# Score matmuls on four parts of the array, with a new order of the token pipeline, two buffers for h and staggered first weights

## What is computed

```
x = x + layernorm(attention(layernorm(x)))
x = x + layernorm(experts(layernorm(x)))

attention, token by token: 16 heads, 32 + 16 (rotary) numbers each; the scores are head against head
    within one token:  einsum("bsid,bsjd->bsij", q, k), softmax over j, einsum("bsij,bsjd->bsid", attn, v), @ Wo + bo
    q from a latent of 128, k and v from another; rotary part of k from x
experts: 64 experts of width 192, the best 6 for each token, at most 128 tokens to an expert,
    plus a shared gate/up/down of width 384
```

## Time and profile before

| | |
|---|---|
| median of 3 runs | 2026.46 us (2020.72 to 2035.89) |
| profiled execution | 2029.77 us, span 2027.8 us |
| TensorE, VectorE, ScalarE, GpSimd busy | 93%, 75%, 54%, 27% of the span |
| granted TensorE clock, mean | 0.975 |
| DMA packets | 414103, 289704 of them under 512 B |

### The profile page before, as it was taken

One profiled execution on the slowest core, in us unless ns is written; L12 is line 12 of the kernel. 1 busy time (PEld: TensorE's weight loads), 2 busy tenths in 40 slices (PEclk: granted clock), 3 DMA queues, 4 the chain that ended last, 5 costly groups with the idle time before them and its releaser, 6 DMA issues. The chain is left out here.

```text
span 2027.8 us, 49115 instructions
## 1 busy us (share of the span) xinstructions
PE 1893.7 (93%) x14529; PEld 1504.8 (74%) x14529; DVE 1520.7 (75%) x3935; ACT 1091.5 (54%) x1745; POOL 550.1 (27%) x773
## 2 busy tenths in 40 slices
PE   5899999999999999999999999985899999988886
PEld 4788888888888888888888888874454555546664
DVE  6588888888888888888888888773444444429997
ACT  4576767666666767666666767651222233223333
POOL 1111112111111112111111111110344444427776
PEclk8799999999999999999999999997899999999998
DMA  5245454545454454545455554437999999979994
GB/s 189 69 129 147 128 153 129 151 128 150 124 143 138 133 150 128 150 129 152 126 140 137 137 146 128 140 108 222 334 299 284 274 310 307 291 202 394 406 398 171
DMA packets 414103, 383.99 MB, mean 189 GB/s; under 512 B 289704, under 2 KB 298024, under 8 KB 413992
## 3 DMA queue, kind: packets, MB, share of 16 engines
q1 hardware_dynamic: 393504, 324.98, 53.1%
q0 software_dynamic: 14336, 35.66, 7.5%
q10 hardware_dynamic: 6208, 22.68, 2.9%
HBM read 232.46 MB, written 150.63 MB: 189 GB/s over the span
## 5 line engine op out<-in xcount | busy, mean ns | idle before, releaser
L861 POOL TENSOR_SCALAR ve<-mv 128x1 f32<-128x1 f32 x192 | 42.7, 222 | 1073.1 <-DVE mv L698 1072.3
L593 ACT COPY qT<-bank 48x512 f32<-48x512 f32 x256 | 269.1, 1051 | 72.2 <-PE bank L445 67.6
L593 ACT COPY kT<-bank 48x512 f32<-48x512 f32 x256 | 268.8, 1050 | 4.8
L1068 PE MATMUL e_gu<-w,xgT 128*128 128x384 f32 x512 | 184.3, 503 | 15.4 <-DMA w<-w_ed 13.5
L452 PE MATMUL bank<-wgu,xfT 128*128 128x416 f32 x512 | 189.1, 369 | 8.3 <-ACT xfT L593 8.3
L453 PE MATMUL bank<-wgu,xfT 128*128 128x416 f32 x512 | 183.5, 358 | 0.0
L642 ACT ACTIVATE prob<-prob 128x512 f32<-128x512 f32 x128 | 78.7, 633 | 176.3 <-DVE prob L795 176.3
L469 PEld LDWEIGHTS score_ps<-kT,qT 48*64 48x64 f32 x4096 | 133.4, 138 | 40.7 <-issue 40.7
L469 PE MATMUL score_ps<-kT,qT 48*64 48x64 f32 x4096 | 151.1, 225 | 11.5 <-ACT kT L593 11.5
L1068 PEld LDWEIGHTS e_gu<-w,xgT 128*128 128x128 f32 x512 | 93.2, 192 | 74.7 <-DMA w<-w_ed 14.2
L1229 DVE SCALAR_TENSOR_TENSOR tanh<-tanh,e_gu 128x192 f32<-128x192 f32 x64 | 22.7, 354 | 166.3 <-ACT tanh L1155 166.3
(11 more groups left out here) (177 smaller groups left out, 4922.8 us busy)
## 6 DMA issues: line engine op xcount, KB each, us to landing
w<-w_eg SPq DMA_DIRECT2D x60, 768.0 KB, 6.7
acc_scratch<-zero SPq DMA_DIRECT2D x130, 256.0 KB, 4.2
w<-w_ed SPq DMA_DIRECT2D x60, 384.0 KB, 11.0
xf_scratch<-xf SPq DMA_DIRECT2D x64, 288.0 KB, 2.1
xin<-x SPq DMA_DIRECT2D x64, 256.0 KB, 2.9
v_scratch<-v SPq DMA_DIRECT2D x64, 256.0 KB, 3.7
vbd<-v_scratch SPq DMA_DIRECT2D x128, 128.0 KB, 3.2
o_scratch<-o SPq DMA_DIRECT2D x256, 64.0 KB, 2.3
```

The costliest lines, as they stand in the source:

```text
L593: nc.scalar.copy(dst, src).then_inc(done.sem, 1)
L1068: last = nc.tensor.matmul(gu_ps[par], xgT[:, par, n, :], w1[:, place, n, :], start=(n == 0), stop=(n == KD - 1))
```

## The change

Six things change together. (1) q and k go to SBUF on two sets of partitions, 0 to 47 and 64 to 111, for the first and the last 64 tokens of a tile; `scores` then has matmuls on four parts of the array (two of rows, r, by two of columns, g), all 32 in one piece, the two row parts writing to different banks. `spread` makes 16 copies of 48 x 256 for 8 of 48 x 512. q is laid out by (head, token) within four tokens, so o's partitions are (head, token), and the mask changes to p % B4. (2) o is written to memory in that order, and oin is read back by four DMAs, one for each token of the four, each of 32 partitions x 16 x 32 numbers, where there was one DMA of 128 x 512. (3) TensorE's order: the latent product is split into its high part and its low part, with the transposes of k between; q's product goes ahead of the gate/up products; the second gate/up half goes behind the transposes of oin; xn is transposed ahead of prob; the rank matmul goes last. (4) The orders of ScalarE and VectorE follow; yn becomes VectorE's last. (5) h has two buffers. (6) The first experts' weights are asked for one expert a round, in the rounds NT + 1 to NT + 4.

The diff, cut to its core:

```diff
-    c[:, C_NEG:C_NEG + B4] = np.where((p[:, None] // H) % B4 == np.arange(B4), 0.0, -BIG)
+    c[:, C_NEG:C_NEG + B4] = np.where(p[:, None] % B4 == np.arange(B4), 0.0, -BIG)
...
-        qT, kT = qT_all[0:DQ], kT_all[0:DQ]
+        qT = qT_all[:, 0:P // 2, :].rearrange("p (c x) y -> p c (x y)", x=B4).rearrange("p c (h t) -> p c h t", t=B4)
+        kT = kT_all[:, 0:P // 2, :]
...
-        h = sb("h", [P, SI])
+        h = sb("h", [P, 2, SI])
...
-                    dst = o_d[1 - par].rearrange("(c g b t) (h d) -> g b (t h) c d", c=8, g=2, b=2, h=H)
+                    dst = o_d[1 - par].rearrange("(c g b) (x d) -> g b x c d", c=8, g=2, b=2, d=DH)
                     src = o[:].rearrange("p (c b d) -> p b c d", c=8, b=2)
                     for g in range(2):
                         for b in range(2):
                             sp.dma_start(dst[g, b], src[64 * g:64 * g + 64, b]).then_inc(o_out.sem, 16)
                     sp.wait_ge(o_out.sem, o_out.at(i - 3))
+                    settle(sp)
                     sp.wait_ge(pe_oT.sem, pe_oT.at(i - 4))
-                    sp.dma_start(oin[:], o_d[1 - par]).then_inc(o_in.sem, 16)
+                    settle(sp)
+                    src = o_d[1 - par].rearrange("c (h t d) -> t c h d", t=B4, d=DH)
+                    for n in range(B4):
+                        sp.dma_start(oin[n:P:B4, :].rearrange("p (h d) -> p h d", d=DH), src[n]).then_inc(o_in.sem, 16)
...
-            def scores(blocks):
-
-                for blk in blocks:
-                    for g in range(2):
-                        t0 = (blk // 2) * 16 + g * 8 + (blk % 2) * B4
-                        last = nc.tensor.matmul(score_ps[64 * g:64 * g + 64, blk * 64:blk * 64 + 64],
-                                                qT[:, t0:t0 + B4, :].rearrange("p t h -> p (t h)"),
-                                                kT[:, t0:t0 + B4, :].rearrange("p t h -> p (t h)"),
+            def scores():
+
+                for blk in range(NBLK // 2):
+                    four = (blk // 2) * 4 + blk % 2
+                    for g, r in ((0, 0), (1, 1), (1, 0), (0, 1)):
+                        c4 = four + 2 * g
+                        part = slice(64 * r, 64 * r + DQ)
+                        at = r * 512 + blk * 64
+                        last = nc.tensor.matmul(score_ps[64 * g:64 * g + 64, at:at + 64],
+                                                qT[part, c4].rearrange("p h t -> p (h t)"),
+                                                kT[part, B4 * c4:B4 * c4 + B4, :].rearrange("p t h -> p (t h)"),
                                                 start=True, stop=True)
...
                 def spread(dst, src, done, n):
 
-                    dv = dst.rearrange("p t (m a) -> p a m t", a=2)
                     for a in range(2):
-                        copy(dv[:, a, 4 * n:4 * n + 4, :],
-                             src[64 * a:64 * a + DQ, :].rearrange("p (m t) -> p m t", t=P), done)
+                        sv = src[64 * a:64 * a + DQ, :].rearrange("p (m r c t) -> p r m c t", m=4, r=2, t=B4)
+                        for r in range(2):
+                            copy(dst[64 * r:64 * r + DQ, a, 4 * n:4 * n + 4], sv[:, r], done)
...
-                if isinstance(i, int) and i == NT + 2:
+                if isinstance(i, int) and 0 <= i - NT - 1 < NW:
                     act.wait_ge(pe_k.sem, pe_k.at(NT - 1))
                     settle(act)
-                    for e in range(NW):
-                        load_expert(act, e, e)
+                    load_expert(act, i - NT - 1, i - NT - 1)
...
-            def gated(i, n, b):
+            def gated(i, par, n, b):
 
                 dve.wait_ge(a_th.sem, a_th.at(i - 5, n + 1))
-                dve.wait_ge(h_out.sem, h_out.at(i - 6))
+                dve.wait_ge(h_out[1 - par].sem, h_out[1 - par].at(i - 7))
...
+                if active(i - 3):
+                    dve.wait_ge(g_x1.sem, g_x1.at(i - 4))
+                    normalise(1, yn[:], y[:], i - 3)
             pipeline(dve, iteration)
```

More of the change, by code:

```diff
@@ L491, in iteration @@
                     pe.wait_ge(d_q.sem, d_q.at(i - 2))
-                    product(b5, [xT[:, :, n, :] for n in range(KD)], [wlat[:, :, n, :] for n in range(KD)], d_xT, i, pe_lat)
+                    high(*latents)
+                if active(i - 2):
+                    pe.wait_ge(d_k.sem, d_k.at(i - 2))
+                    pe.wait_ge(d_lat.sem, d_lat.at(i - 2))
+                    pe.wait_ge(a_qT.sem, a_qT.at(i - 2, 4))
+                    turn(k[:, par], pe_kT, 0, b3)
+                    pe.wait_ge(d_xT.sem, d_xT.at(i))
+                    turn(k[:, par], pe_kT, 1, b2)
+                if active(i):
+                    pe.wait_ge(d_xT.sem, d_xT.at(i))
+                    low(*latents, pe_lat)
                 if active(i - 5):
@@ L539, in iteration @@
                                 d_latT, i - 1, pe_q)
+                if active(i - 5):
+                    pe.wait_ge(a_xfT.sem, a_xfT.at(i - 5))
+                    pe.wait_ge(a_qT.sem, a_qT.at(i - 2))
+                    pe.wait_ge(d_y.sem, d_y.at(i - 4))
+                    product(b7[:, 0:GU], normed, [wgu[:, :, n, 0:GU] for n in range(KD)], d_xfT, i - 5, pe_gu)
+                if active(i - 2):
+                    pe.wait_ge(a_kT.sem, a_kT.at(i - 2))
+                    pe.wait_ge(d_xfT.sem, d_xfT.at(i - 5))
+                    pe.wait_ge(a_pT.sem, a_pT.at(i - 3))
+                    pe.wait_ge(a_rank.sem, a_rank.at(i - 6))
+                    settle(pe)
+                    scores().then_inc(pe_s.sem, 1)
+                if active(i - 3):
+                    pe.wait_ge(o_in.sem, o_in.at(i - 3))
+                    pe.wait_ge(a_kT.sem, a_kT.at(i - 2, 4))
+                    transposes(b3, [oin[:, n * P:(n + 1) * P] for n in range(KD)], pe_oT)
+                if active(i - 5):
+                    pe.wait_ge(d_q.sem, d_q.at(i - 1, 1))
+                    pe.wait_ge(d_pv.sem, d_pv.at(i - 3))
+                    product(b4[:, 0:GU], normed, [wgu[:, :, n, GU:] for n in range(KD)], d_xfT, i - 5, pe_gu)
                 if active(i - 3):
                     pe.wait_ge(a_oT.sem, a_oT.at(i - 3))
+                    pe.wait_ge(a_qT.sem, a_qT.at(i - 2))
                     pe.wait_ge(d_h.sem, d_h.at(i - 5, 2))
-                    pe.wait_ge(d_r.sem, d_r.at(i - 5, 2))
+                    pe.wait_ge(d_r.sem, d_r.at(i - 5, 1))
                     product(b7, [oT[:, :, n, :] for n in range(KD)], [wo[:, :, n, :] for n in range(KD)], d_oT, i - 3, pe_wo)
@@ L548, in iteration @@
                     transposes(b3, [lat[:, n * P:(n + 1) * P] for n in range(2)], pe_latT)
+                if active(i + 1):
+                    pe.wait_ge(d_ln[0].sem, d_ln[0].at(i + 1))
+                    pe.wait_ge(a_kT.sem, a_kT.at(i - 2))
+                    transposes(b2, [xn[:, n * P:(n + 1) * P] for n in range(KD)], pe_xT)
                 if active(i - 2):
@@ L557, in iteration @@
                     product(b6, [latT[:, 1 - par, :, 1, :]], [wck[:, :, 0, :]], d_latT, i - 1, pe_k)
-                if active(i + 1):
-                    pe.wait_ge(d_ln[0].sem, d_ln[0].at(i + 1))
-                    pe.wait_ge(a_kT.sem, a_kT.at(i - 2, 4))
-                    transposes(b2, [xn[:, n * P:(n + 1) * P] for n in range(KD)], pe_xT)
-                if active(i - 5):
-                    pe.wait_ge(d_r.sem, d_r.at(i - 5, 7))
-                    pe.wait_ge(a_pT.sem, a_pT.at(i - 2))
-                    nc.tensor.matmul(rank_ps, chosen[:], tri[:], start=True, stop=True).then_inc(pe_rank.sem, 1)
                 if active(i - 2):
@@ L577, in iteration @@
                     last.then_inc(pe_pv.sem, 1)
+                if active(i - 5):
+                    pe.wait_ge(d_r.sem, d_r.at(i - 5, 7))
+                    pe.wait_ge(a_pT.sem, a_pT.at(i - 2))
+                    nc.tensor.matmul(rank_ps, chosen[:], tri[:], start=True, stop=True).then_inc(pe_rank.sem, 1)
             pipeline(pe, iteration)
```

188 lines of the change are left out of this document (86 added, 102 removed).

## The result

| | before | after |
|---|---|---|
| median of the runs (11 each) | 2029.5 us | 2038.9 us |
| range | 2018.4 to 2035.9 | 2032.4 to 2050.3 |
| ratio | | 1.0055, 95% interval [1.0034, 1.0075] |
| span of the profiled execution | 2027.8 us | 2032.2 us |
| one round (52 rounds between two k's) | 20.70, standard deviation 0.03 | 20.81, standard deviation 0.34 |

The kernel became slower, as forecast, but by 9.4 us and not by 38. That is inside the range and within 1% of no change, where the forecast had put a chance of 0.17.

A forecast was written before the change was run, and what follows sets the result against it. TensorE's full queue bounds the kernel at 20.70 us a round; afterwards the loop through o, at 21.4. About 59 rounds x 0.7 = +41, ends -3: 2068, or 2065 us on the scale of medians; range 2012 to 2108.

The forecast's parts named there:

- The bound moves from TensorE's queue to the loop through o: Loop oin, TensorE, k, o, write, read-back grows to 21.4 us a round; TensorE waits 1 to 1.7 for oin.
- The scores, 1.08 saved: TensorE's 64 score records on four array parts take about 1.08 us, saving 1.08 a round.
- The leg of SyncE: End of o to oin landed, through write and read-back: from 7.0 to 8.7 us with four reads.
- The leg from oin to k: TensorE from oin's transposes to the key product's end, 8.0 us, plus 0.2 to VectorE's k.
- The leg on VectorE: From k to the end of o: 5.24 us less 0.68 as yn leaves, 4.56.
- the second rival: About the same: loop as forecast but its unknowns low, landing 2.2; round 20.8 to 21.0; chance 0.17.
- The first one: Faster rival: oin's read-back no longer than TensorE's queue allows; round 20.3, near 2000 us; chance 0.13.
- The third: Rival, slower by ScalarE's copies: all 16 at 0.61 us, scores end behind oin; 22.1 a round, near 2105; chance 0.10.
- The fourth, the clock: Rival: TensorE's idling drops its clock each round, 1.7 us of work; 23.1 a round, near 2165; chance 0.06.
- VectorE's new wait for x1: With yn at VectorE's end, the second statistics wait 0.8 us a round for POOL's x1.
- The ends: First and last rounds: spread expert weights and two h buffers give back 3 to 5 us; together -3.

The follow-up runs named there:

- yn back: Changed kernel with yn put back behind the key sum k on VectorE, all else as changed: 2096.3 us, ratio 1.0317 to the kernel before.
- the old order: Changed kernel with VectorE's whole old order between k and o (yn and xT's low part back there): 2197.3 us, ratio 1.0806 to the kernel before.
- xT's low part outside: Changed kernel with xn's transposes back behind the key product and xT's low part behind o on VectorE: 2009.9 us, ratio 0.9904 to the kernel before.
- one read: Changed kernel with oin read as whole rows in one DMA instead of four, tokens mixed up: 1988.1 us, ratio 0.9789 to the kernel before.
- the run with the rows apart: Changed kernel with all score matmuls of the first row part ahead of the second's: 2058.1 us, ratio 1.0118 to the kernel before.
- xn's transposes behind: Changed kernel with xn's transposes back behind the key product on TensorE: 2043.0 us, ratio 1.0085 to the kernel before.
- k first: Changed kernel, xn's transposes behind the key product, xT's low part behind o, k ahead of the choice and latT's low part: 2012.3 us, ratio 0.9896.
- the new order alone: Kernel before with only yn moved behind o on VectorE; scores, read-back and ends as before: 2024.4 us, ratio 0.9971.

## Why the prediction was right and wrong

- **The bound moves from TensorE's queue to the loop through o: right.** TensorE waits for oin in each of 58 rounds, and each edit that changed the length of the loop moved the round: longer with yn back and with the old order, shorter with xT's low part outside or with one read. In the kernel before the same order changed nothing.
- **The scores, 1.08 saved: right** (64 records in 1.16), and right that the saving is spent in the wait for oin: half of it by the run with the rows apart.
- **The leg of SyncE, forecast 8.7, was 9.16.** The four reads were asked 0.65 apart as forecast (1.95 from the first to the last). From the last of them to the transposes 2.79 passed, where I had taken 2.4, with 2.43 as the smallest and 3.68 as the largest of 52. The loop has no slack, so each late landing goes into the round: that is the standard deviation of 0.34.
- **The leg from oin to k, forecast 8.2, was 8.00: right, but half of the picture.** I had it end with the key product, and TensorE's part was 7.93 where I had 8.0, the step to k 0.10 where I had 0.2. What I had not seen is a second path as long: VectorE's queue behind y, with statistics, choice, latT's low part, then k. It made no difference to the time, but it is why the leg stayed at 8.06 with xn's transposes behind, and fell only with k first (7.52).
- **The leg on VectorE, forecast 4.6, was 3.65. This is the term that was mis-sized**, by 0.9 us a round, 59 x 0.9 = 54 us. I took away yn's slot and kept the rest as it was: the term for what else the move changes between k and o stood at nothing, without a reason. But yn's going also moved GpSimd's x1, which starts behind it, away from xf (0.70), and saved a wait at srec (0.11) and 0.08 more in yn's slot. The run with the old order brought xf's 0.9 back with the overlap, and the three odd rounds of the run with yn back show it within one kernel.
- With the three legs as measured, 21.5 (the sum of the forecast's legs) - 0.95 + 0.46 - 0.2 = 20.8, against 20.81 measured. That the kernel became slower at all, as forecast, is in part luck: with VectorE's leg as measured the forecast's own 21.4 would have been 20.45, faster than the 20.70 of before, and only the read-back, 0.46 longer than I had it, put the round above it again.
- **The rivals.** The time was the second rival's (20.8 to 21.0), but not its reason: the landing came out high, not low. The first one's price for a short read-back holds where it was tried: 20.18 and 1988 with one read. The third did not happen: the copies of q took 367 ns and those of k 604, and TensorE did not wait for kT. By the Trainium skill (SBUF — State Buffer, Specifications (TRN2)) the q copies, with several accesses to one 16-byte line, take the low price and the k copies the high one; the trace agrees, with these two numbers. The fourth, the clock, did not come in the kernel after, with waits of 0.6, and did in the old order, with waits of 2.1. It came by degrees: in 2 of 56 rounds with a mean wait of 0.9 (xn's transposes behind), 7 of 54 with 1.3 (yn back), 44 of 50 with 2.1. I had its price at 1.7 a fall; it was 1.53.
- **VectorE's new wait for x1, forecast 0.8**, was 0.7 and cost nothing, until y's statistics were moved and it stood ahead of something that was waited for.
- **The ends, forecast -3**: not settled, the sign likely.

## What to carry to other kernels

Before a full queue is made shorter, walk the loops through memory that run beside it, leg by leg, instruction by instruction; the change pays only down to the longest of them, and a leg that grows is paid in full. An instruction that takes far longer than its size can be a sign of a neighbour on another engine, so moving one thing can change the duration of another that stays. Changing places within a loop gains nothing by itself: move work out of it, and then look for what stands in the queue ahead of the next thing awaited. Where two paths end at the same instruction, both have to be shortened.

## What the runs showed of the hardware

- **VectorE and GpSimd.** A scaling of 128x64 numbers in SBUF took 0.25 us alone and 0.95 when it started inside GpSimd's 1.27-us sum, ending with it; the mean of its group was 911 ns before, 254 after, 898 in the old order, 256 in the new order alone. With yn put back it took 0.25 when it started first and 1.3 when the sum had started 0.03 earlier. xT's low part, which reads a PSUM bank, ran beside the same sum at its usual 0.68. The Trainium skill (SBUF — State Buffer, SBUF: two separate sides) has one port pair that the two engines share as an exclusive lock, which VectorE needs only for some of its instructions, and whichever starts first blocks the other for its whole instruction; the traces agree, in that xf waited for the sum's end and xT's low part did not.
- **Small matmuls on four parts of the array.** 64 records of 48x64 in 1.16 us are 18 ns each, or 36 for each of the 32 matmuls, which have two records. In the trace the records come in groups of four, one for each part, which start 6 to 7 ns apart, and from group to group pass 59 ns; before, the same 59 ns passed from pair to pair. The Trainium skill (TensorE: Matmul & The Clock Gate, Wait — 56ns, not 53.3ns?) says that starts are never closer than about 25 ns, which would make 1.6 for 64; the mean by matmul, 36, would not go against that, but the starts 6 to 7 ns apart do, and the measurement decides. With the two row halves not alternating it was 1.91, 30 ns each.
- **The clock.** With 0.6 us of waiting in each round of 20.8 the granted clock stayed at 1.00; with 2.1 in each of 23.6 it fell to 0.50 (1.2 GHz) in 44 of 50 rounds, and that cost about as much (1.35 a round) as VectorE's longer leg (1.31).
- **A DMA of 128-byte pieces** held SyncE's queue 0.65 us where one of whole rows, four times its size, held it 0.34.
